# Macaron block (gated recurrence, delta-rule scan, gated recurrence): reciprocal roots by power on GpSimd, one gate product, reworked first norm and last tile

## What is computed

```python
def ffn(x, ...):                      # scan over the first axis, 8 steps, c of (1024, 256)
    def step(c, xt):
        ft = sigmoid(xt @ wf.T + c @ uf.T + bf)
        it = sigmoid(xt @ wi.T + c @ ui.T + bi)
        gt = tanh(xt @ wc.T + c @ uc.T + bc)
        return ft * c + it * gt, None
    c_final, _ = lax.scan(step, c0, x)
    return tanh(einsum('tbi,oi->tbo', x, wo) + c_final @ uo.T + bo)

def attn(x, ...):                     # 16 heads of 16, scan over 1024 tokens, batch 8
    static_out = x @ W.T
    k = q = rmsnorm(x by head, k_norm_w)
    o_dyn = gated_delta_rule_scan(q, k, -static_out, sigmoid(lam_logit), beta_neg)
    return layernorm(static_out + o_dyn, o_norm_w, o_norm_b)

x = x + 0.5 * ffn(layernorm(x))
x = x + attn(layernorm(x))
x = x + 0.5 * ffn(layernorm(x))
```

## Time and profile before

| what | value |
|---|---|
| median of 3 runs | 1371.61 us (1363.8 to 1374.17) |
| the profiled execution's own time | 1371.25 us |
| its span | 1369.5 us |
| PE busy (matmul) | 1263.5 us, 92% |
| DVE busy | 878.1 us, 64% |
| ACT busy | 666.4 us, 49% |
| POOL busy | 269.5 us, 20% |

### The profile page before, as it was taken

How to read it: one execution, slowest core, us unless ns; L and a number is a source line. 1 busy time by engine, 2 the same in 40 slices (tenths; PEclk the granted TensorE clock), 3 DMA queues, 4 the chain that set the end, 5 groups by cost and what they waited for, 6 DMA issues and landing times.

```text
span 1369.5 us, 58093 instructions
## 1 busy us (share of the span) xinstructions
PE 1263.5 (92%) x25763; PEld 1167.3 (85%) x25763; DVE 878.1 (64%) x2147; ACT 666.4 (49%) x1623; POOL 269.5 (20%) x350
## 2 busy tenths in 40 slices
PE   6999999999999999998898899899899999999896
PEld 5989998989989888787777788888789989898886
DVE  3656886868879676577658764953445546464632
ACT  3244444454434535544463555355365756655432
POOL 0113112021311111112503230230130405050500
PEclk9999999999999999999998999999999999999999
DMA  4010201122121223242214223324234233333000
GB/s 146 1 62 32 65 33 66 64 80 73 42 80 50 102 68 92 67 140 66 83 47 162 65 74 117 92 77 138 73 95 150 65 112 102 109 102 108 1 32 31
DMA packets 72378, 108.36 MB, mean 79 GB/s; under 512 B 12352, under 2 KB 49472, under 8 KB 70080
## 3 DMA queue, kind: packets, MB, share of 16 engines
q1 hardware_dynamic: 72128, 104.65, 23.9%
HBM read 53.74 MB, written 50.86 MB: 76 GB/s over the span
## 4 chain that ended last, share of the span: by engine, by line
PE 67%; DVE 18%; ACT 8%; issue 5%; DVEq 0%; ACTq 0%
PE ps L445 37%; PE ps L512 7%; PE ps L868 5%; PE ps L1058 4%; PE ps L1075 3%; ACT gates L462 3%; PE ps L675 3%; ACT zbd L1092 2%; DVE prod L790 2%; DVE inv L793 2%; DVE ln_bn L83 2%; PE ps L405 2%; PE ps L704 1%; DVE hs L526 1%; DVE ffn_rows L537 1%
## 5 line engine op out<-in xcount | busy, mean ns | idle before, releaser
L445 PE MATMUL ps<-cst,wt 128*128 128x128 f32 x2688 | 348.7, 282 | 3.5 <-DVE cst L490 3.4
L445 PEld LDWEIGHTS ps<-cst,wt 128*128 128x128 f32 x2688 | 318.7, 194 | 14.6 <-DVE cst L490 4.1
L445 PE MATMUL ps<-ffn_rows,wt 128*128 128x128 f32 x2304 | 295.7, 281 | 10.8 <-DVE hs L526 4.1
L445 PEld LDWEIGHTS ps<-ffn_rows,wt 128*128 128x128 f32 x2304 | 275.9, 194 | 20.8 <-issue 13.2
L462 ACT ACTIVATE gates<-ps,colv 128x128 f32<-128x128 f32 x448 | 128.0, 369 | 188.7 <-PE ps L445 188.5
L484 DVE TENSOR_TENSOR fc<-gates,cst 128x256 f32<-128x256 f32 x112 | 56.1, 501 | 223.5 <-ACT gates L462 223.5
L1161 POOL TENSOR_TENSOR ffn_rows<-ffn_rows,rowv 128x256 f32<-128x256 f32 x64 | 52.0, 851 | 351.3 <-DMA ffn_rows<-x_scratch 351.3
L1092 ACT ACTIVATE zbd<-ps,mask 32x256 f32<-32x256 f32 x252 | 104.0, 458 | 10.7 <-PE ps L1075 7.6
L868 PE MATMUL ps<-inv_cols,kv 32*32 32x32 f32 x8192 | 88.7, 194 | 18.5 <-issue 16.9
L868 PEld LDWEIGHTS ps<-inv_cols,kv 32*32 32x32 f32 x8192 | 79.2, 104 | 30.5 <-issue 20.9
L445 PE MATMUL ps<-kg_rows,wt 128*128 128x128 f32 x768 | 95.1, 278 | 6.6 <-DVE hs_more L526 3.5
(11 more groups left out here) (123 smaller groups left out, 1793.7 us busy)
## 6 DMA issues: line engine op xcount, KB each, us to landing
xs_scratch<-xs_out SPq DMA_DIRECT2D x32, 512.0 KB, 3.5
xsb<-xs_scratch SPq DMA_DIRECT2D x256, 64.0 KB
ffn_rows<-x SPq DMA_DIRECT2D x32, 256.0 KB, 3.6
x_scratch<-ffn_rows SPq DMA_DIRECT2D x32, 256.0 KB, 2.8
kg_scratch<-kg_rows SPq DMA_DIRECT2D x32, 256.0 KB, 2.8
kgb<-kg_scratch SPq DMA_DIRECT2D x256, 32.0 KB, 2.3
e_scratch<-e SPq DMA_DIRECT2D x256, 32.0 KB
ffn_rows<-e_scratch SPq DMA_DIRECT2D x8, 1024.0 KB
```

What stands on the lines that cost most here:

```text
L445: mm = pe.matmul(banks[g][:, col:col + P], wt[:, w, k, m * P:(m + 1) * P], rhs, start=(x in (0, FI)), stop=(k == KT - 1 and (t == 0 or x > ...
```

## The change

1. `LayerNorm.coefficients_bn` goes. DVE keeps statistics and aggregation (`moments_bn`); POOL makes x = var + eps, a = -mean, rs = x ** -0.5 by a two-input operation with a broadcast column of -0.5, and nm = a * rs (`coefficients_pool`, `LN_OPS` 4). The rms piece likewise goes to POOL: one multiply-add and one power on 128x128.
2. The state moves into the third quarter of `gates`, doubled, so that fc and ig are one 128x512 product `fcig` for t > 0.
3. The first block's norm is found and applied in two halves (`first_half_bn`, still Newton on DVE); PE's fills 2 and 3 and the tables move behind step 0; the first gate weights have a semaphore of their own, and the block boundary is gone.
4. In the last block `pe_h` goes to banks 4 to 7 and is issued one half per step, DVE's last operations are reordered, and the last store is four stores.

The diff, cut:

```diff
 RSQRT_OPS = 11
-LN_OPS = RSQRT_OPS + 1
+FIRST_OPS = RSQRT_OPS + 1
+LN_OPS = 4
...
-    def coefficients_bn(self, dve, n, stats):
+    def moments_bn(self, dve, n, stats):
         link = Link(dve, self.bn_done, 16 * n + 8)
         link.wait()
+        wait_pos(dve, self.found, LN_OPS * (n - self.first))
         for b in range(8):
             link(dve.bn_aggr(stats[:, b, 6:8], stats[:, b, 0:6]))
+
+    def coefficients_pool(self, pool, n, stats, exponent):
+        pool.wait_ge(self.bn_done, 16 * n + 16)
+        wait_pos(pool, self.applied, 8 * n)
+        link = Link(pool, self.found, LN_OPS * (n - self.first))
+        link(pool.tensor_scalar(self.x, stats[:, :, 7], 1.0, LN_EPS, ALU.mult, ALU.add))
+        link(pool.tensor_scalar(self.a, stats[:, :, 6], -1.0, 0.0, ALU.mult, ALU.add))
         link.wait()
-        wait_pos(dve, self.applied, 8 * n)
-        link = Link(dve, self.found, n * LN_OPS)
-        rsqrt(dve, link, self.rs, self.x, self.a, stats[:, :, 7], LN_EPS, 1.0, range(RSQRT_OPS))
+        link(pool.tensor_tensor(self.rs, self.x, exponent.to_broadcast([P, B]), ALU.pow))
         link.wait()
-        link(dve.scalar_tensor_tensor(out=self.nm, in0=stats[:, :, 6], scalar=-1.0, in1=self.rs,
+        link(pool.tensor_tensor(self.nm, self.a, self.rs, ALU.mult))
...
-        gates = [sb(f"gates{q}", [P, 3, D]) for q in range(2)]
+        gates = [sb(f"gates{q}", [P, 4, D]) for q in range(2)]
+        cst = [gates[q][:, 2, :] for q in range(2)]
+        fcig = sb("fcig", [P, 2, D])
...
             def h_b(self, b):
+                if self.last(b):
+                    return ps[4:8]
...
                 if 1 in parts:
-                    dve.tensor_tensor(ig, gates[q][:, 1, :], gates[q][:, 2, :], ALU.mult).then_inc(self.products, 1)
-                    dve.tensor_tensor(cst, fc, ig, ALU.add).then_inc(self.c_done, 1)
+                        dve.tensor_tensor(fcig, gates[q][:, 0:2, :], gates[q][:, 2:4, :], ALU.mult).then_inc(self.products, 2)
+                    dve.tensor_tensor(cst[(t + 1) % 2], fcig[:, 0, :], fcig[:, 1, :], ALU.add).then_inc(self.c_done, 1)
...
+            elif name == "rms":
+                link = Link(pool, ms_done, n * MS_OPS + 1)
+                link.wait()
+                link(pool.tensor_scalar(rms, rms, 1.0 / HD, RMS_EPS, ALU.mult, ALU.add))
+                link.wait()
+                link(pool.tensor_tensor(rms, rms, minus_half.to_broadcast([P, P]), ALU.pow))
...
             if u == 2:
+                ln3.coefficients_pool(pool, n, bn_buf[1], minus_half)
                 pool.wait_ge(x1_in[p], b.landed)
...
+            if u == 5:
+                fg.ln.coefficients_pool(pool, n, bn_buf[2], minus_half)
...
                     if f is not None and t < 7:
                         f.pe_step(pe, b, t + 1, 3 * part, 3 * part + 3)
+                        if f.last(b) and part == 3 and t > 0:
+                            f.pe_h(pe, b, (t - 1) // 2, ((t - 1) % 2,))
...
+                if t == 1 and n == NB - 1:
+                    for j in range(4):
+                        sp.wait_ge(fg.x_done, 4 * n + j + 1)
+                        sp.dma_start(out_v[n][:, 2 * j:2 * j + 2, :], xt[n % 2][:, 2 * j:2 * j + 2, :]).then_inc(o_out[n % 2], 16)
...
+        def setup_act(act):
+            act.activation(sc[:, 1:2], lanev[:, 1:2], ACT.Tanh).then_inc(ca, 1)
+            ff.ln.apply_first(act, first_found, 0, xn, xt[0])
+            ff.act_front(act, Block(0), (0, 1))
+            ff.ln.apply_first(act, first_found, 1, xn, xt[0])
+            act.wait_ge(cs, 1)
```

More of the change, by code:

```diff
@@ L98, in apply_pool, with apply_first @@
+    def apply_first(self, act, found, half, dst, src):
+        tiles = range(4 * half, 4 * half + 4)
+        act.wait_ge(found, FIRST_OPS * (half + 1))
+        for b in tiles:
+            act.activation(dst[:, b, :], src[:, b, :], ACT.Identity, bias=self.nm[:, b:b + 1],
+                           scale=self.rs[:, b:b + 1]).then_inc(self.applied, 1)
     def apply_pool(self, pool, n, dst, src, tiles):
-        pool.wait_ge(self.found, (n + 1) * LN_OPS)
+        pool.wait_ge(self.found, (n + 1 - self.first) * LN_OPS)
@@ L502, in pe_h @@
             def pe_h(self, pe, b, j, halves=(0, 1)):
-                if j == 0 and 0 in halves:
+                h_b = self.h_b(b)
+                if self.last(b):
+                    if 0 in halves:
+                        pe.wait_ge(bank[4 + j].read, LAST_READ[4 + j])
+                        pe.wait_ge(z_done, STATE_OPS * (HOPS - 1))
+                elif j == 0 and 0 in halves:
                     pe.wait_ge(self.fi_read, 8 * b.n + 8)
-                h_b = self.h_b(b)
                 if 0 in halves and h_b[j] is self.g_b(b)[-1]:
@@ L593, in prep_dve @@
                 link(dve.tensor_reduce(rms, by_head(key_half[:, 0:BD]), AX.X, ALU.add))
-            elif name == "rms":
-                dve.wait_ge(ff.x_done, 4 * (n + 1))
-                link = Link(dve, ms_done, n * MS_OPS + 1)
-                link.wait()
-                rsqrt(dve, link, rms, rms_x, rms_a, rms, RMS_EPS, 1.0 / HD, range(RSQRT_OPS))
             elif name == "key":
@@ L1201, in second_pe @@
                 for r in range(2):
-                    if done is not None:
+                    if done is not None and not old.last(done):
                         old.pe_h(pe, done, 2 + r)
@@ L1218, in second_pe @@
                         f.pe_step(pe, b, t + 1, 3 * part, 3 * part + 3)
+                        if f.last(b) and part == 3 and t > 0:
+                            f.pe_h(pe, b, (t - 1) // 2, ((t - 1) % 2,))
+                    elif f is not None and f.last(b):
+                        if part < 2:
+                            f.pe_h(pe, b, 3, (part,))
                     elif f is not None:
@@ L1286, in second_dve @@
                     f.dve_step(dve, b, t, (1,))
-                if done is not None:
+                if done is not None and old.last(done):
+                    for j in range(4):
+                        old.dve_x(dve, done, j)
+                        if j < 2:
+                            old.dve_h(dve, done, j + 2)
+                elif done is not None:
                     for j in (2, 3) if old is ff else range(4):
@@ L1491, in _ @@
[L1491 to L1503 removed]
+                setup_sp(sp)
```

193 lines of the change are left out of this document (108 added, 85 removed).

## The result

The changed kernel takes 1462.9 us (median of 4 runs, 1461.4 to 1463.8), the kernel before 1370.3 us beside it (1363.8 to 1374.2): a ratio of 1.0705, 95% interval 1.0665 to 1.0745 (the two medians divided give 1.0676, inside it). The forecast was 1356 us and a range up to 1369, so it was wrong, and wrong in sign. The profiled execution has a span of 1459.6 us.

The account below looks back on a forecast made before the run. PE, 92% busy, was taken to bound the kernel, with DVE setting a few stretches. Gains of 21.3 us less 5.8 given back made 15.5 us, so 1371.25 us would become 1356 us, range 1341 to 1369.

Parts of the forecast that it names:

- the price p: Length of POOL's 128x128 rms power: taken as 2.5 us, giving back 5.8 us in blocks 7 and 8.
- the rival's formula: Very long power, key on DVE waiting in blocks 1 to 8: slower from p = 9.6, 1386 us at 12; chance 0.12.
- 21.3 us of gains: All gains over the kernel, 22.3 us less 1 us kept back for waits that show up next.
- L801, 9.2 + 2.3 us: PE's L851 waits behind DVE's rms root: 9.2 us in blocks 7 and 8 with slow clock, 2.3 in 1 and 6.
- zbd, 5.3 us: PE's waits for zbd: 3.4 us from the 2.72 us wait, 0.9 in block 8, 1.0 in block 9.
- 1.5 us of slow clock: Behind the 2.72 us zbd wait: lost clock that goes, since a remaining 0.8 us wait is too short to bring it.
- L704, 1.1 us: PE's L704 waits behind DVE's norm coefficients ahead of g0, t=7 of blocks 2 to 5: 1.1 us gained.
- The gate product: For t > 0 one 128x512 product, about 0.7 us, replaces 0.42; fc no longer stands in front of zbd.
- The start, 2.4 us: First x part at 18.8, 3.4 us sooner, less 1.0 us for eight transposes moved into step 0.
- The end, 1.0 us: Last block: last c part 5.6 us later, last store piece 2.8 us; 1.0 us gained in all.
- The small powers, "room everywhere": The norms' 128x8 powers on POOL: coefficients were ready some 12 us or about 5 us before use.
- The long-power rival: Power of 5.6 to about 10 us delaying blocks 7 and 8: result 1363 to 1371 us; chance 0.12.

Follow-up runs that it names:

- rms_on_dve: The changed kernel with the 128x128 rms root back on DVE as a Newton chain, the layer norms' powers still on POOL; 1358.9 us, ratio 0.9971.
- only_rms_pool: The kernel before with only the rms root moved to POOL as a power; 1464.4 us, ratio 1.0762.
- newton_on_pool: The changed kernel with the rms root still on POOL, but as 14 plain Newton passes in place of the power; 1364.1 us, ratio 0.9977.
- power_64: The changed kernel with the rms power on 64 of the 128 columns, no root taken of the others; 1376.1 us (one run).
- newton_on_pool_ahead: newton_on_pool with the root ahead of the post adds in step 4 on POOL; 1352.7 us, ratio 0.9875.
- adds_first: rms_on_dve with its Newton chain behind tt0 in step 4, and POOL's eight post-step adds at u=2 ahead of the norm power; 1378.6 us.
- no_power: rms_on_dve with the layer norms' coefficients also as Newton chains on DVE, so no power at all; 1359.6 us, ratio 0.9975.

## Why the prediction was wrong

**The step that failed is the price p.** The prediction: "if the power is worked out like the Newton chain, in eleven plain passes of that kind, 11 x 0.51 = 5.6 us, and nothing in the trace excludes more. I take 2.5 us." It is 20.7 us, 3.7 times the upper bound. The bound was no bound: it came from supposing how a power is computed, and not from any row of a power. The sentence said so, and the range still ended at p = 8. What the runs showed in its place: with this one operation back as a Newton chain on DVE the loss is gone (rms_on_dve), alone in the kernel before it makes all of it (only_rms_pool), and with 14 plain passes in its place on the same engine there is none (newton_on_pool).

**The mechanism was right, and the rival's formula nearly.** With p = 20.7 the prediction's own line gives 21.3 - 2 x 21.1 - 12.3 - 5 x 10.2 = -84 and so 1455; measured 1462.9. Block by block: 2 x 21.1 = 42.2 for blocks 7 and 8, measured waits 19.4 + 19.8 = 39.2; 12.3 for block 6, measured 9.7 at zbd and 2.0 at the transposes behind it; 51 for blocks 1 to 5, measured 42.9. PE noticed there at the transposes of the keys (L728), not at c as I wrote, and at about the same p, as power_64 has no such wait. The "every further us costs 8" is the 8.0 to 8.5 of the runs. That the formula's total comes within 7 us is in part luck. It has the waits 11.7 us too long (105.5 against 93.8). It has nothing for the slow clock behind them, and its 21.3 us of gains even hold 4.3 us of clock given back, where PE's busy time rose by 12.8. And it lacks the 5.0 us wait for the last norm. The first error hides about half of the other two. That rival had 0.12, with "it would be some twenty plain passes" against it: it is as long as some forty.

**The gains were about right.** The ten new waits come to 91.8 + 2.0 + 5.0 = 98.8 us, and PE's idle time grew by 77.3: so 21.5 us of other waits went. In time, newton_on_pool_ahead shows the gains best, as nothing long waits for the root there: 17 us (12 to 22 by the interval) with the 5.0 us wait still against it, where 21.3 were forecast. In the changed kernel the clock is the part that gave nothing: PE's matmuls took 12.8 us more, since the new waits bring slow matmuls of their own.
- *L801, 9.2 + 2.3 us:* the waits are gone in the changed kernel, as forecast, and stay (9.6 us) in rms_on_dve. It is the one gain that needs the root off DVE. newton_on_pool_ahead has it, and by the ratios (0.9875 and 0.9971) it is 13 us under rms_on_dve, 7 to 19 with the intervals: 11.5 lies within.
- *zbd, 5.3 us:* right in place; rms_on_dve has only 0.6 us of them left. Of the two causes that the prediction named, the adds beside the inverse are shown: adds_first puts them back in front, with no norm chain on DVE, and 4.2 + 3.1 us of zbd waits return. The gate product shows nothing here: no_power keeps it, has the adds in front again, and waits 2.65 us in block 7 where the kernel before waited 2.72. Of the 1.5 us of slow clock the rows show 0.9 (1.94 us of transposes against 1.06), and behind the 2.65 us wait of no_power the transposes took 1.06, so that term did not hang on the wait's length as forecast. Whether the norm chains on DVE add to these waits isn't shown: no run takes them off with the adds in front and the order of step 4 unchanged.
- *L704, 1.1 us:* these waits are 2.8 us before, 3.6 in no_power and 1.7 in rms_on_dve, so the norm chains cause 1.1 to 1.9 us of them, about as much as I took.
- *The gate product:* forecast 0.7 us, measured 0.69; contended 1.55 (at 125.57, beside the keys).
- *The start, 2.4 us:* forecast 18.8, less 1.0. Measured 19.04, less 1.04, so 2.1. The other transposes are where they were expected:

```profile
19.04 4.57 PE L479 MATMUL ps<-ffn_rows,wt 128*128 128x128 f32 x24 [0.77 <-ACT ffn_rows L448]
...
23.45 1.04 PE L439 MATMUL ps<-ident,ffn_rows 128*128 128x128 f32 x8
```

- *The end, 1.0 us:* the last c part ends 11.8 us before the span's end, 18.2 before, less 5.6 for the six halves put ahead of it: 0.8. The last piece of the output, by the timeline of the end:

```profile
1444.99 2.84 PE L479 MATMUL ps<-gates,wt 128*128 128x128 f32 x24
...
1455.53 1.47 DVE L576 SCALAR_TENSOR_TENSOR ffn_rows<-hs_more,ffn_rows 128x512 f32<-128x512 f32 x2
```

it is written at 1457.0, and 2.6 us later the span ends, where 2.8 were forecast.
- *The small powers, "room everywhere":* wrong once. In the post step at u=2 POOL used to do its eight adds while DVE was at the statistics; with the power on POOL the adds wait for them too, and the last block's norm comes some 4 us late. The prediction asked only whether the coefficients had room, and put the 6.2 us of adds queued behind them at nothing; in adds_first the wait is 0.7 us.

*Slips in the sums.* The long-power rival gives back 2 x 6.0 us at p = 5.6, not 2 x 6.4, and at p = 8 its formula gives 1366.8 us, not 1366. The 3.6 us by which the sum would be better with p at its lower end go with p = 0.7, while 0.5 gives 4. None of these matters beside p.

**What stays open.** How much slow clock belongs to each of the new waits isn't settled, nor what each of the other gains is worth in time: start, end and the waits at L704 were read from the traces, and no run has one of them alone.

## What to carry to other kernels

Where the price of an operation isn't in the trace, the case is decided by that price and not by the care put into the rest: if nothing excludes ten times the estimate, then the chance of the rival that needs it may not be 0.12. A chain of plain passes whose price is known can be better than one operation whose price isn't; here 14 passes of 0.3 to 0.5 us on GpSimd beat one power of 20.7 us. And an engine that is little used is not free at every moment: on GpSimd it mattered more what stood ahead of the new work (adds that cost some 11 us of wait in each of blocks 7 and 8) and behind it (6.2 us of adds) than how busy it was.

## What was new of the hardware

- GpSimd's power operation costs 1.65, 5.42, 10.52 and 20.73 us for 8, 32, 64 and 128 f32 columns on 128 partitions: 0.16 us a column and about 0.3 us fixed, by these four. A plain product of 128 columns on the same engine takes 0.40 to 0.46 us, a multiply-add 0.30. The Trainium skill, "GPSIMD Engine Reference", section 3.1, gives some 2.6 cycles per element for a two-input add; the prediction's estimate from it, 0.28 us and a fixed cost, agrees with the plain product's 0.40 to 0.46 us. The power, the same instruction with another operation, is 45 to 52 times as long as that product. So that figure belongs to the operation measured, and not to the form of the instruction.
- DVE's plain pass on 128x128 took 0.29 us where nothing ran beside it, and 0.55 to 0.78 beside GpSimd's adds (block 7 of rms_on_dve):

```profile
648.59 0.72 DVE L62 TENSOR_TENSOR hs<-rms 128x128 f32<-128x128 f32 x1
...
650.47 0.29 DVE L62 TENSOR_TENSOR hs<-rms 128x128 f32<-128x128 f32 x1
```

So the same chain is worth more when moved off DVE than its quiet length: between the sums and L801 it stood 5.7 us in block 7 of the kernel before, and 3.4 us in block 2.
